# A cross-attention kernel whose output bias is copied into the accumulator bank by ScalarE instead of being multiplied in by TensorE

## What is computed

```python
Q = (x @ w_q.T)   K = (ctx @ w_k.T)   V = (ctx @ w_v.T)      # 16 heads of 32
scores = einsum('bhqd,bhkd->bhqk', Q, K) / sqrt(32)
ctx = einsum('bhqk,bhkd->bhqd', softmax(scores), V)           # 64 keys for each batch
out = ctx @ w_o.T + b_o
x = out + query
return (x - mean(x)) * rsqrt(var(x) + eps) * ln_gamma + ln_beta
```

## Time and profile before

| | before |
|---|---|
| time, median of 3 runs (lowest, highest) | 612.33 us (609.22, 612.86) |
| time of the profiled execution | 616.87 us |
| its span, first to last instruction | 615.1 us |
| mean granted TensorE clock | 0.977 |
| PE, DVE, ACT, POOL busy, share of the span | 95%, 77%, 73%, 77% |
| the chain that ended last: PE, DVE, ACT, DMA | 81%, 6%, 4%, 4% |

### The profile page before, as it was taken

The page is one execution under the profiler, slowest core; times in us unless marked ns, Lnnn a source line. Parts: engine busy times, 40 slices in busy tenths (PEclk is TensorE's granted clock), DMA queues, the critical chain, the costliest instruction groups (busy, mean ns, idle before and its releaser), DMA issues.

```text
span 615.1 us, 12235 instructions
## 1 busy us (share of the span) xinstructions
PE 582.4 (95%) x4330; PEld 462.0 (75%) x4330; DVE 472.7 (77%) x874; ACT 450.3 (73%) x799; POOL 476.6 (77%) x333
## 2 busy tenths in 40 slices
PE   8888889998999999999999999998999999999875
PEld 7655558887877888788868788886888877888553
DVE  7857348876888888888868888886888877888657
ACT  7657467867877788888777888885888777877831
POOL 4627347886988888988878888897789888878840
PEclk9989889998999999999989999998999999999988
DMA  8342213332343333433334233333334423122323
GB/s 308 126 91 58 57 42 96 95 91 92 114 116 87 114 103 104 121 115 91 102 97 120 85 109 113 102 115 88 100 104 118 114 84 93 55 71 74 108 85 120
DMA packets 79757, 62.74 MB, mean 102 GB/s; under 512 B 52272, under 2 KB 52272, under 8 KB 79696
## 3 DMA queue, kind: packets, MB, share of 16 engines
q1 hardware_dynamic: 79696, 61.96, 33.9%
HBM read 39.39 MB, written 16.78 MB: 91 GB/s over the span
## 4 chain that ended last, share of the span: by engine, by line
PE 81%; DVE 6%; ACT 4%; DMA 4%; issue 3%; SPq 1%; POOL 1%; ACTq 0%; DVEq 0%
PE ps_q L425 23%; PE ps_o L431 23%; PE ps_c L473 13%; PE ps_s L368 6%; DMA out<-y 4%; PE ps_o L393 3%; PE ps_o L307 3%; PE ps_s L307 3%; PE ps_s L379 3%; PE ps_q L307 2%; SPq L287 1%; ACT inverse L582 1%; DVE q_lo L634 1%; DVE turned L721 1%; DVE half_max L727 1%
## 5 line engine op out<-in xcount | busy, mean ns | idle before, releaser
L817 POOL TENSOR_TENSOR p_lo<-probs,p_hi 128x1024 fp32r<-128x1024 f32 x59 | 142.2, 2410 | 67.3 <-ACT p_hi L515 67.3
L425 PE MATMUL ps_q<-x_hi,wq_lo 64*128 64x512 f32 x448 | 179.1, 400 | 6.2 <-DVE q_lo L634 6.2
L431 PE MATMUL ps_o<-wo_hi,c_lo 64*128 64x512 f32 x448 | 179.1, 400 | 0.0
L431 PE MATMUL ps_o<-wo_lo,c_hi 64*128 64x512 f32 x448 | 178.2, 398 | 0.0
L425 PE MATMUL ps_q<-x_lo,wq_hi 64*128 64x512 f32 x448 | 177.4, 396 | 0.0
L425 PE MATMUL ps_q<-x_hi,wq_hi 64*128 64x512 f32 x448 | 176.9, 395 | 0.0
L431 PE MATMUL ps_o<-wo_hi,c_hi 64*128 64x512 f32 x448 | 176.8, 395 | 0.0
L425 PEld LDWEIGHTS ps_q<-x_hi,wq_lo 64*128 64x128 f32 x448 | 83.5, 186 | 17.8 <-DVE q_lo L634 10.5
L721 DVE STREAM_TRANSPOSE turned<-ps_s 128x1024 f32<-128x1024 f32 x64 | 80.0, 1251 | 14.1 <-PE ps_s L368 9.8
L431 PEld LDWEIGHTS ps_o<-wo_lo,c_hi 64*128 64x128 f32 x448 | 84.0, 188 | 8.4
L425 PEld LDWEIGHTS ps_q<-x_hi,wq_hi 64*128 64x128 f32 x448 | 83.8, 187 | 8.6
(11 more groups left out here) (123 smaller groups left out, 1436.2 us busy)
## 6 DMA issues: line engine op xcount, KB each, us to landing
xT_raw<-in_xT SPq DMA_DIRECT2D x64, 256.0 KB, 3.0
x_raw<-in_x SPq DMA_DIRECT2D x64, 256.0 KB, 2.9
out<-y SPq DMA_DIRECT2D x64, 256.0 KB, 2.2
max_rows<-max_turned SPq DMA_DIRECT2D x128, 16.0 KB
ctx_raw<-in_ctxT SPq DMA_DIRECT2D x4, 256.0 KB, 5.0
wk_raw<-in_wkT SPq DMA_DIRECT2D x4, 256.0 KB, 5.3
wq_raw<-in_wqT SPq DMA_DIRECT2D x4, 256.0 KB, 6.0
wv_raw<-in_wvT SPq DMA_DIRECT2D x4, 256.0 KB, 7.3
```

Of the source, the lines that this page charges most:

```text
L425: return nc.tensor.matmul(ps_q[:, 0, :], w[l][half, k, dims], x_[r][half, qc % 2, k, :], start=(half is lower and k == 0 and step == 0), s ...
L431: return nc.tensor.matmul(ps_o[:, 0, :], cx[l][half, k, tile], wo[r][half, k, :], start=False, stop=(half is lower and k == KT - 1 and ste ...
L817: nc.gpsimd.tensor_tensor(p_lo[:, :, :], probs_of(n)[:, :, :], p_hi[:, :, :].bitcast(fp32), ALU.subtract).then_inc(p_lo_done, 1)
```

## The change

The bias now comes into a tile's bank by ScalarE. The vector is loaded once, spread over all 128 partitions, into a new tile `bias_row`, and `put_bias(i)` copies that tile (128 by 512) into the output bank of tile i. The products of `project_both` and `project_output` add onto it. `start_output` is gone from TensorE, and with it what prepared `signs` and `max_rows`: one load and one small transfer of SyncE, two operations of GpSimd, two fills of VectorE, and four waits. `put_bias(i)` waits for what `start_output(i)` waited for, and TensorE waits for `bias_done` ahead of the tile. SyncE no longer waits for `bias_added`. The load of the bias stands in SyncE's iteration 5, ahead of those of gamma and beta, and waits there until all four value products are done (`values_product`), since `bias_row` lies where weights of the first stage lay.

```diff
-            sp.dma_start(inverse[96:128, :], b_o.partition_broadcast(32)).then_inc(bias_loaded, 16)
...
-            sp.wait_ge(bias_lo_done, 1)
-            sp.dma_start(max_rows[97:98, :].bitcast(fp32), inverse[97:98, :]).then_inc(bias_filled, 16)
...
                 if t == 5:
+                    sp.wait_ge(values_product, KT)
+                    sp.dma_start(bias_row[:, :], b_o.partition_broadcast(P)).then_inc(bias_loaded, 16)
                     for row, src in ((gamma_row, gamma), (beta_row, beta)):
...
                     wait(sp, shifted_done, t)
-                    wait(sp, bias_added, t - OUT_LAG + 2)
...
-            def start_output(i):
-                if i == 0:
-                    pe.wait_ge(ones_filled, 1)
-                    pe.wait_ge(values_lo_done, KT)
-                if i <= TILES - G:
-                    wait(pe, z_done, i)
-                elif i >= TILES - G + 2:
-                    pe.wait_ge(exp_done, SLOTS)
-                else:
-                    pe.wait_ge(q_lo_done, SLOTS)
-                nc.tensor.matmul(out_bank(i), signs[64:128, :, :].rearrange("p a i -> p (a i)"),
-                                 max_rows[64:128, :], start=True, stop=False).then_inc(bias_added, 1)
-
             def wait_context(i):
+                pe.wait_ge(bias_done, i + 1)
...
             def project_output(i):
                 c, t = divmod(i, G)
                 rows = slice(t * P, (t + 1) * P)
+                pe.wait_ge(bias_done, i + 1)
...
                     subtract_max(t - 1)
-                    start_output(i + 1)
                     combine_values(t - 2, True)
...
-                if i == -1:
-                    start_output(0)
...
-                if 0 <= i < TILES - 1:
-                    start_output(i + 1)
...
+            def put_bias(i):
+
+                if i == 0:
+                    act.wait_ge(bias_loaded, 16)
+                    act.wait_ge(values_lo_done, KT)
+                    act.wait_ge(first_vbd_lo_done, 4)
+                if i <= TILES - G:
+                    wait(act, z_done, i)
+                elif i >= TILES - G + 2:
+                    act.wait_ge(exp_done, SLOTS)
+                else:
+                    act.wait_ge(q_lo_done, SLOTS)
+                nc.scalar.activation(out_bank(i), bias_row[:, :], ACT.Copy).then_inc(bias_done, 1)
...
                 if t + 1 < SLOTS:
                     queries_to_hi(t + 1)
+                if 0 <= t - OUT_LAG + 1 < TILES:
+                    put_bias(t - OUT_LAG + 1)
...
-            dve.wait_ge(consts_done, 1)
-            nc.vector.memset(signs[64:128, :, :].bitcast(fp32), 0.0).then_inc(ones_zeroed, 1)
-            dve.wait_ge(ones_zeroed, 1)
-            nc.vector.memset(signs[96:98, :, :].bitcast(fp32), 1.0).then_inc(ones_filled, 1)
...
-            pool.wait_ge(bias_loaded, 16)
-            pool.wait_ge(x_lo_done, KT)
-            nc.gpsimd.tensor_copy(max_rows[96:128, :], inverse[96:128, :]).then_inc(bias_hi_done, 1)
-            pool.wait_ge(bias_hi_done, 1)
-            nc.gpsimd.tensor_tensor(inverse[96:128, :], inverse[96:128, :], max_rows[96:128, :].bitcast(fp32),
-                                    ALU.subtract).then_inc(bias_lo_done, 1)
-            pool.wait_ge(bias_lo_done, 1)
```

More of the change, by code:

```diff
@@ L102, in cross_attention_kernel @@
             c_lo[odd] = sb(f"c_lo{odd}", [P, G, CHUNK], fp32r)
-        y = sb("y", [P, 2, DM], fp32)
+        y, bias_row = sb("y", [P, 2, DM], fp32), sb("bias_row", [P, DM], fp32)
         def ps(name, banks):
@@ L233, in _ @@
                             "p (k h i) -> p k h i", k=2, h=2)[:, :, head, :],
-                            signs[0:1, part, :].bitcast(fp32).rearrange("p (k i) -> p k i", k=2)).then_inc(select_filled, 16)
+                            signs[0:1, part, :].rearrange("p (k i) -> p k i", k=2)).then_inc(select_filled, 16)
             for u in range(KT, SPLIT_AHEAD + 3):
@@ L302, in _, with three_passes @@
         def _(pe):
-            def three_passes(dst, pairs, first=True, last=True):
+            def three_passes(dst, pairs, first=True, last=True, onto=False):
                 passes = [p for (l_hi, l_lo), (r_hi, r_lo) in pairs
@@ L307, in three_passes @@
                     mm = nc.tensor.matmul(dst, lhs, rhs, start=(first and n == 0),
-                                          stop=(last and n == len(passes) - 1))
+                                          stop=(last and n == len(passes) - 1), skip_group_check=onto)
                 return mm
@@ L409, in project_output @@
                                                      (wo_hi[:, k, :], wo_lo[:, k, :]))],
-                                      first=False, last=(k == KT - 1))
+                                      first=False, last=(k == KT - 1), onto=True)
                 mm.then_inc(o_product, 1)
@@ L430, in output @@
                     l, r = ((1, 0), (0, 1), (0, 0))[step]
-                    return nc.tensor.matmul(ps_o[:, 0, :], cx[l][half, k, tile], wo[r][half, k, :],
-                                            start=False, stop=(half is lower and k == KT - 1 and step == 2))
+                    return nc.tensor.matmul(ps_o[:, 0, :], cx[l][half, k, tile], wo[r][half, k, :], start=False,
+                                            stop=(half is lower and k == KT - 1 and step == 2), skip_group_check=True)
                 if not second:
```

14 lines of the change are left out of this document (4 added, 10 removed).

## The result

The changed kernel takes 640.6 us (median of 4 runs, 634.5 to 642.0) against 611.8 us of the kernel before beside it. The ratio is 1.046, with an interval of 1.038 to 1.053. So it is slower by 29 us, where the prediction had 10 us and a range that ended at 631.

A forecast was written before the change was run, and what follows sets the result against it. ScalarE's loops were taken to bound the kernel, with TensorE and `q_lo` also near their limit. 7.0 + 1.6 + 2.8 - 2.0 + 0.9 = +10.3 us on 612.33 gave 622.6 us (stated 622.5), range 611 to 631.

The forecast's parts named there:

- The regular cycle: Steady part, 54 cycles: the cycle becomes 8.43 us by the longer loop instead of 8.30, +7.0 us.
- the one by the store: Steady cycle, from one exponential through logarithm, `y`, `q_hi` and the copy to the next: sum 8.36 us.
- The loop by `z`: Steady cycle, from one exponential through logarithm, `half_max`, `z` and the copy to the next: sum 8.43 us.
- rival B: Steady part: copy cheap at 0.40 us, late stores no worse, the ends take the loss back; 613 us, chance 0.27.
- Over the ten or so late ones this is +1.6 us: Late stores, steady part: about 0.15 us of each delay, swallowed today by TensorE's work, goes through in full.
- I count half of four: Middle delays of late stores: half of four lose TensorE's clock at 1.4 us each, +2.8 us, ends 0 and 5.6.
- nothing that I can derive: Steady part: said of how often a store lands late; long waits for stores gone or doubled would show it wrong.
- The start: First tiles: ScalarE's logarithm comes at 86.5 instead of 88.51 us; -2.0 us, between -1.0 and -2.6.
- The end: Last tiles: exponential waits for `z` and the copy, +1.4 us; lost bias products -0.5 us; together +0.9 us.
- A: Steady part: ScalarE has slack, TensorE's gain comes through up to `q_lo`; -8.1 us there, 603 us, chance 0.12.
- C: Steady part: TensorE's clock falls in every cycle from a 0.5 us wait; +75.6 us, 688 us, chance 0.03.
- the 8.15 us: Steady cycle as set by TensorE and `q_lo` if ScalarE does not hold it: 8.30 - 0.15 us.

The follow-up runs named there:

- after_y3: The changed kernel with three buffers for `y` instead of two: 603.3 us, ratio 0.987 to the kernel before.
- before_dummy: The kernel before, TensorE's bias product kept, plus a 128x512 ScalarE copy into an unread tile in the bias copy's place: 633.0 us, ratio 1.031.
- store_first: The changed kernel with SyncE issuing the output store ahead of the wait for the maximum and its two transfers: 604.1 us, ratio 0.986.
- after_cyc: The changed kernel with three already satisfied waits added to each shared iteration of TensorE: 636.3 us, ratio 1.043 to the kernel before.
- no_bias_y3: The changed kernel without bias product or copy (bias left out of the result) and with three buffers for `y`: 585.7 us, ratio 0.960.

## Why the prediction was wrong

**The regular cycle** was right: +0.09 us forecast as +0.13, 8.395 for 8.43, +4.9 us for +7.0. The exponential came at 1.40 us behind `z`, not 1.27, and the loop that holds is the one by the store, 8.36 in the sum and 8.39 measured. The loop by `z` was 0.18 us too long in the sum: `after_y3`, in which it alone is left, runs at 8.25. The steps in it were 1.03 + 4.89 + 1.24 us from the exponential to `z`. In the rows above, the logarithm at 159.68 is 4.84 us ahead of `half_max` at 164.52, and that 1.13 us ahead of `z`. I had added the full 1.21 us of `half_max` and 0.03 us, but `z` starts 0.08 us before the record of `half_max` ends; the other 0.05 us were idle time of the old cycle. The copy, read off `x_hi` at 0.52 us of ScalarE's time, measured 0.52 us from start to start (166.53 to 167.05). A copy into SBUF takes 0.622 us (`before_dummy`) and the one into the bank 0.594. The Trainium skill ("ScalarE: Activation LUTs", "Step-by-step: what each stage is for") has ScalarE reach PSUM faster than SBUF; the runs agree, by 0.03 us, far from the 0.1 of rival B.

**The step that failed is that of the late stores**, "Over the ten or so late ones this is +1.6 us" and "I count half of four". The mechanism was right and is seen in the rows: each delay goes through in full, and some of them cost the clock. What failed is the count. The step kept the late stores of before, and 3 over 2 us became 10. The clock fell seven times and not three, where I had counted two falls more. By the medians and the excess it measured +18.6 us in place of 1.6 + 2.8 = +4.4. The prediction named it as "nothing that I can derive", but gave it no width: the range's upper end held a dearer copy and more clock drops, not more late stores. What could have been read before the change is that a late store needs a second thing, a fetch of instructions, at a certain distance behind the issue; and that in the kernel before ten of its fetches lay at 1.7 to 2.35 us, just behind the harmful distance, where a store later by 0.44 us comes nearer to them (the fetches moved as well, which those rows don't tell). I had seen neither, since I took the late stores for scatter.

**The start** was forecast at -2.0 us and came at +1.0. ScalarE's logarithm did get free, but TensorE then waited at its first shared iteration, and `q_hi` behind it, which answers to the earlier trace rows:

```profile
84.97 0.60 ACT L534 ACTIVATE ps_o<-bias_row 128x512 f32<-128x512 f32 x1 [1.01 <-issue]
...
87.21 0.76 PE L408 MATMUL ps_q<-x_hi,wq_lo 64*128 64x512 f32 x1 [2.35 <-POOL wo_lo L820]
...
96.17 0.60 ACT L493 ACTIVATE q_hi<-ps_q 128x512 fp32r<-128x512 f32 x1 [5.06 <-PE ps_q L408]
```

TensorE had no bias product to wait at any more, came to the next wait earlier, and this was GpSimd's split of the output weights, which nothing had made earlier. I followed ScalarE there and left GpSimd out. Even so the first shared iteration began 1.06 us earlier than before (87.21 and 88.27 us). What lost that and more is the clock that I had named and not priced: from 87.2 to 90.6 us TensorE was granted 0.50 and to 94.0 us 0.75, where before it had 0.89 in the first 3.4 us of that iteration and 1.00 in the next. `q_hi` came 1.06 us later (96.17 and 95.11).

**The end** was forecast at +0.9 us and came at -0.2. The exponential does wait for `z` and the copy, as written, which answers to the earlier trace rows:

```profile
599.25 0.60 ACT L534 ACTIVATE ps_o<-bias_row 128x512 f32<-128x512 f32 x1 [0.78 <-DVE z L739]
599.78 1.01 ACT L620 ACTIVATE probs<-ps_s 128x1024 f32<-128x1024 f32 x1
```

The last four tiles took that back: counted from the last `z` of the steady part, the kernel after is 2.2 us behind the one before at the `z` of tile 59, and 0.2 us ahead at that of tile 63. It is more than the 0.5 us that I gave them, and how much of it is the missing products I did not work out.

**The rivals.** *A* (ScalarE has slack, 603 us) is false here, and is what happens as soon as the store no longer holds ScalarE: 603 and 604 us in `after_y3` and `store_first`. It had the right number for another kernel. *B* is false, the copy was not cheap. *C* is false in its form: with a short wait in each cycle (0.35 us by the 8.045 us in which TensorE never waits) the median cycle stays at 8.395 us, and cycles over 11.5 us stand only behind late stores, seven of them. The Trainium skill's warning there ("TensorE: Matmul & The Clock Gate", "A second HAM failure mode: psum-queue depth-cycling") is not borne out for waits this short.

**What stays open.** Why nine fetches begin at 6.7 to 7.3 us behind `z` after the change, where ten were at 7.1 to 7.6. Twelve instructions at the start of TensorE's list move them, so that they depend on where TensorE stands in it; but a list brought back to the length of before did not bring them back (`after_cyc`), and a kernel whose TensorE list is that of before has four at 6.9 to 7.0, where the kernel before has none (`before_dummy`). That ScalarE's lag moves them through TensorE's waits is an argument and was not tested. Nor is it settled why 2.43 us of waiting cost the clock and 2.02 us did not.

## What to carry to other kernels

Where a profile has one kind of cycle many times and a few long ones, subtract the median and ask of each long one what else moved at that time, the queues that are not your own included: here 18.6 of the 24 us between the two profiled executions came from 16 KB fetches of instructions that met a store in flight, and no row of an engine names them. A wait that ends just in time in every cycle is a trap for every change near it; give it slack first (a third buffer, or the store ahead of transfers that must wait for something else, 604 us without any memory), and measure the change on top. With that slack, moving the bias from TensorE to ScalarE was worth nothing, since the product had cost 0.285 us of a cycle, the copy costs 0.205, and of the difference 0.5 us were left in the time.

## What the runs showed of the hardware

- A 16 KB packet of the instruction queue that begins 1.0 to 1.7 us behind the issue of a 256 KB store delays it in 45 of 45 cases: the `y` that waits for it starts 3.6 to 4.7 us behind the issue and not 2.2 to 2.3. Without such a packet it is 0 of 300. The packet takes 1.0 to 1.9 us, and eight of the store's 128 packets, the share of one of 16 DMA engines, begin only when it ends (41 of the 45).
- 256 satisfied waits in TensorE's stream, 128 instructions, put off the first `z` of the steady part by about 15 us (119.57 against 104.41), some 0.12 us for each instruction.
- In the kernel before, TensorE's output products begin 0.22 us behind its query products on the other half of the rows (median of the cycles; 378.74 and 378.95 us in one), nearly a whole step of 0.23. In the kernel after and in `no_bias_y3` both begin together (167.41 and 167.42; 402.47 both). That may be how `no_bias_y3` beats the 8.15 us, but I did not isolate it.
- A VectorE addition of two 128x512 operands in SBUF took 0.69 us where GpSimd was idle, began later or was about to end, and up to 2.85 us where a GpSimd operation from SBUF was under way: it ended 0.54 to 0.55 us behind that operation's end in 40 of 40 cases.
